# Opening of a graph-network kernel: halved first loads, the mean subtracted in the scaling, GpSimd rounding two weights

## What is computed

```
h  = relu(layernorm(x))                            # 1250 x 1024
e  = sigmoid(h @ wenc.T + benc)                    # 1250 x 500, the "encoder"
a  = segment_sum((e @ conv)[src] * edge_weight, dst) + e @ lin.T
x1 = x + a @ wdec.T + bdec
out = x1 + normalised_adjacency(src, dst) @ (relu(layernorm(x1)) @ W.T + b)
```

## Time and profile before

| | |
|---|---|
| median of 3 runs | 472.21 us (472.15 to 472.41) |
| span of the profiled execution, first to last instruction | 470.4 us |
| PE busy | 464.4 us |
| DVE busy | 284.1 us |
| ACT busy | 198.8 us |
| POOL busy | 109.3 us |
| granted TensorE clock, mean over the span | 1.000 (2.4 GHz) |

### The profile page before, as it was taken

How to read it: one execution, slowest core, us unless ns; L and a number is a source line. 1 busy time by engine, 2 the same in 40 slices (tenths; PEclk the granted TensorE clock), 3 DMA queues, 4 the chain that set the end, 5 groups by cost and what they waited for, 6 DMA issues and landing times.

```text
span 470.4 us, 7573 instructions
## 1 busy us (share of the span) xinstructions
PE 464.4 (99%) x3326; PEld 378.2 (80%) x2826; DVE 284.1 (60%) x527; ACT 198.8 (42%) x376; POOL 109.3 (23%) x102
## 2 busy tenths in 40 slices
PE   8999999999999999999999999999999999999997
PEld 6999999988899999888877785444449887777776
DVE  7999797697539259062367885994130095344443
ACT  6899976664439210142024446024342512221210
POOL 1500000000040000000013444000003599896640
PEclk9999999999999999999999999999999999999999
DMA  8620004000000134600499600733310133613113
GB/s 321 246 91 2 1 2 176 2 1 1 2 2 0 4 123 134 239 6 0 147 341 185 96 0 1 309 152 132 131 72 0 57 131 145 227 55 87 44 44 91
DMA packets 26316, 44.70 MB, mean 95 GB/s; under 512 B 15525, under 2 KB 15836, under 8 KB 25638
## 3 DMA queue, kind: packets, MB, share of 16 engines
q1 hardware_dynamic: 26024, 43.77, 28.5%
q0 software_dynamic: 224, 0.39, 0.3%
q10 hardware_dynamic: 30, 0.02, 0.0%
HBM read 27.53 MB, written 13.41 MB: 87 GB/s over the span
## 4 chain that ended last, share of the span: by engine, by line
PE 93%; DVE 4%; DMA 1%; issue 0%; SPq 0%; DVEq 0%
PE ps L1441 89%; PE ps L1445 3%; PE ps L1459 1%; DMA xn<-in_x_dram 1%; DVE zlo L1024 1%; DVE welo L1030 1%; DVE xn L1121 0%; DVE stats L965 0%; DVE stats L966 0%; PE ps L1620 0%; DVE h_all L1035 0%; DVE x1b L1434 0%; DVE kf L1090 0%; DVE mv L968 0%; DVE kb L1084 0%
## 5 line engine op out<-in xcount | busy, mean ns | idle before, releaser
L1441 PE MATMUL ps<-CT,ghi 125*128 125x500 f16 (+1 forms) x240 | 77.0, 339 | 0.0
L1441 PE MATMUL ps<-CT,glo 125*128 125x500 f16 (+1 forms) x240 | 76.9, 339 | 0.0
L1424 DVE SCALAR_TENSOR_TENSOR x1b<-ps,dsc,x1b 125x512 f32<-125x512 f32 x49 | 35.1, 746 | 34.3 <-PE ps L1441 34.2
L646 POOL TENSOR_TENSOR glo<-t,ghi 125x512 f16<-125x512 f32 x18 | 20.6, 1166 | 137.7 <-ACT t L883 137.7
L658 POOL TENSOR_TENSOR S<-U_all 128x500 f32<-128x500 f32 x25 | 31.7, 1277 | 83.8 <-DVE Blo L1398 58.8
L1441 PE MATMUL ps<-A_lo,h2hi 125*125 125x250 f32 (+1 forms) x160 | 49.1, 307 | 0.0
L1441 PE MATMUL ps<-wdhi,h_all 125*125 125x512 f32 (+1 forms) x128 | 40.4, 395 | 0.0
L1441 PE MATMUL ps<-zhi,wehi 128*125 128x250 f32 x160 | 39.4, 289 | 0.2 <-POOL wehi L619 0.2
L1441 PE MATMUL ps<-Bhi,Shi 128*125 128x512 f32 (+1 forms) x144 | 39.3, 388 | 0.0
L1441 PE MATMUL ps<-Blo,Shi 128*125 128x512 f32 (+1 forms) x144 | 39.3, 388 | 0.0
L1441 PEld LDWEIGHTS ps<-CT,ghi 125*128 125x128 f16 x240 | 23.5, 98 | 19.0 <-issue 0.3
(11 more groups left out here) (182 smaller groups left out, 1070.2 us busy)
## 6 DMA issues: line engine op xcount, KB each, us to landing
xn<-in_x_dram SPq DMA_DIRECT2D x10, 512.0 KB, 7.1
x<-in_x_dram SPq DMA_DIRECT2D x10, 512.0 KB
x_scratch<-x SPq DMA_DIRECT2D x10, 500.0 KB
x1b<-x_scratch SPq DMA_DIRECT2D x10, 500.0 KB
out_dram<-x1b SPq DMA_DIRECT2D x19, 240.0 KB
B<-in_W_dram SPq DMA_DIRECT2D x4, 1024.0 KB, 8.0
c_scratch<-C SPq DMA_DIRECT2D x10, 305.2 KB
wd<-in_wdec_dram SPq DMA_DIRECT2D x1, 2048.0 KB, 15.4
```

The source lines that it names most:

```text
L646: p.tensor_tensor(glo[k][0:PB, cs], t32[(2 * k + c) % 4][0:PB, :], ghi[k][0:PB, cs], ALU.subtract).then_inc(*glo_p.up(k, c))
L1424: v.scalar_tensor_tensor(r, ps[bank8["w", u, m]][0:PB, 0:512], scale, r, ALU.mult, ALU.add).then_inc(*term_ok.up(u, m, n))
L1441: return t.matmul(o_ap, lhsT, rhs, start=start, stop=stop)
```

## The change

- Blocks 0 and 1 of x are loaded as four half blocks, each with a semaphore, and `bn_stats` of a half waits for that half alone. The order is (0, 0), (0, 1), (1, 0), (1, 1).
- For blocks 0 and 1, `nb` is not computed. The scaling is (x - mean) * rstd, and waits for `rstd`.
- POOL waits for `rstd` of the first norm step in place of the last scaling. It rounds weights 0 and 1, each when it has landed, and then gathers.
- ACT no longer rounds weight 1. After its counting it goes straight to the four `zhi`.
- On DVE, `wenc_lo(0)` goes ahead of the statistics of block 2.
- The second warm-up has 34 matmuls in place of 45.

```diff
-WARM = (10, 45)
+WARM = (10, 34)
...
-    d_xn = [signal(f"d_xn{i}", [(k,) for k in range(i, NB, NXN)], 16) for i in range(NXN)]
+    d_xn = [signal(f"d_xn{i}", [(k,) for k in range(i if i > 1 else i + NXN, NB, NXN)], 16) for i in range(NXN)]
+    d_half = {(k, h): signal(f"d_half{k}{h}", [()], 16) for k in range(2) for h in range(2)}
...
-    norm_ok = signal("norm_ok", one(len(NORMS)))
+    norm_ok = signal("norm_ok", [(n,) for n in range(1, len(NORMS))])
...
-    whi_p = signal("whi_p", [(0,)])
-    whi_a = signal("whi_a", [(f,) for f in range(1, FB)])
+    whi_p = signal("whi_p", one(2))
+    whi_a = signal("whi_a", [(f,) for f in range(2, FB)])
+
+    def whi_ok(f):
+        return (whi_p if f < 2 else whi_a).at(f)
...
-        load_xn(0)
-        load_xn(1)
+        for (k, h), landed in d_half.items():
+            q.dma_start(xn[k][:, 512 * h:512 * h + 512], x[k][:, 512 * h:512 * h + 512]).then_inc(*landed.up())
         load_we(0)
...
-        p.wait_ge(*relu_v.at(1, 1))
-        p.wait_ge(*d_we[0].at())
-        p.tensor_copy(wehi[0][:, :, :], we32[0][:, :, :]).then_inc(*whi_p.up(0))
+        p.wait_ge(*rstd_ok.at(0))
+        for f in range(2):
+            p.wait_ge(*d_we[f].at())
+            p.tensor_copy(wehi[f][:, :, :], we32[f][:, :, :]).then_inc(*whi_p.up(f))
         for t in range(2):
             gather(t)
...
-        a.wait_ge(*d_we[1].at())
-        a.activation(wehi[1][:, 0:4, :], we32[1][:, 0:4, :], ACT.Copy)
         for k, h in FIRST:
             z_hi(k, h)
-        wenc_hi(1, 4)
         block_mean(3)
...
-            v.wait_ge(*d_xn[k % NXN].at(k))
+            v.wait_ge(*(d_half[k, 0].at() if k < 2 else d_xn[k % NXN].at(k)))
             v.bn_stats(stats[0:PB, k, 0, :], t[0:PB, 0:512])
+            if k < 2:
+                v.wait_ge(*d_half[k, 1].at())
             v.bn_stats(stats[0:PB, k, 1, :], t[0:PB, 512:1024]).then_inc(*x_seen.up(k))
...
-            v.wait_ge(*rstd_ok.at(n))
-            v.scalar_tensor_tensor(col["nb"][0:PB, cs], mv[0:PB, cs, 0], -1.0, d, ALU.mult, ALU.mult).then_inc(*norm_ok.up(n))
+            if n:
+                v.wait_ge(*rstd_ok.at(n))
+                v.scalar_tensor_tensor(col["nb"][0:PB, cs], mv[0:PB, cs, 0], -1.0, d, ALU.mult, ALU.mult
+                                       ).then_inc(*norm_ok.up(n))
...
-        v.wait_ge(*norm_ok.at(0))
+        v.wait_ge(*rstd_ok.at(0))
         for k, h in FIRST:
             part = xn[k][0:PB, 512 * h:512 * h + 512]
-            v.tensor_scalar(part, part, col["rstd"][0:PB, k:k + 1], col["nb"][0:PB, k:k + 1], ALU.mult, ALU.add
+            v.tensor_scalar(part, part, mv[0:PB, k, 0:1], col["rstd"][0:PB, k:k + 1], ALU.subtract, ALU.mult
                             ).then_inc(*relu_v.up(k, h))
         find_windows(0)
         find_windows(1)
+        wenc_lo(0)
         norm_stats(2)
-        wenc_lo(0)
```

More of the change, by code:

```diff
@@ L715, in block_var, with wenc_hi @@
                          accum_out=mv[0:PB, k, 1:2]).then_inc(*sums_ok.up(k, "var"))
-        def wenc_hi(f, k0=0):
+        def wenc_hi(f):
             a.wait_ge(*d_we[f].at())
-            a.activation(wehi[f][:, k0:KB, :], we32[f][:, k0:KB, :], ACT.Copy).then_inc(*whi_a.up(f))
+            a.activation(wehi[f][:, :, :], we32[f][:, :, :], ACT.Copy).then_inc(*whi_a.up(f))
         def z_relu(k, h):
@@ L1028, in wenc_lo @@
         def wenc_lo(f):
-            v.wait_ge(*(whi_a if f else whi_p).at(f))
+            v.wait_ge(*whi_ok(f))
             v.tensor_tensor(welo[f][:, :, :], we32[f][:, :, :], f32(wehi[f][:, :, :]), ALU.subtract).then_inc(*wlo_ok.up(f))
@@ L1477, in enc @@
             o_ap = slot_bank(s)[0:PB, 0:GN]
-            t.wait_ge(*(whi_a if f else whi_p).at(f))
+            t.wait_ge(*whi_ok(f))
             def one_pass(k, kind, start, stop):
```

## The result

| | before | after |
|---|---|---|
| median time | 472.15 us (471.89 to 472.41, 5 runs) | 474.74 us (473.62 to 475.14, 5 runs) |
| span, median | 470.2 us (469.9 to 470.3) | 472.6 us (471.5 to 473.0) |
| time outside the span | 1.9 us | 2.1 us |
| granted TensorE clock | 0.998 to 1.000 | 0.996 to 1.000 |

One more execution of it, at 1,628 us, is left out of every comparison.

What follows compares the result with a forecast made beforehand. PE is busy nearly throughout, so when DVE reaches its last `zlo` sets the time. Halved loads -0.4, no `nb` -0.2, POOL's roundings +1.75 make +1.15; 472.21 + 1.1 = 473.3 us, range 471.3 to 473.8.

Steps and rivals of the forecast that it cites:

- What bounds the kernel: Whole kernel: PE is busy 464.4 of 470.4 us, so only how early DVE reaches its last `zlo` counts.
- no idle time in which to catch up: PE behind 28.47 us: if DVE comes later, PE is later by just that.
- The halved loads: Loads of x blocks 0 and 1: second statistics of block 1 begin earlier, gain 0.4 us, between nothing and 0.64.
- the 0.24 for the later landing of the last bytes: Half loads of x: 0.24 us set as loss for pieces of 2 KB, against 0.64 saved at the most.
- the 0.6 taken as the worst case: Half loads of x: at the stores' rate for 2 KB pieces, the two blocks take 3.27 us against 2.66.
- ahead of the weights: SP's queue: two DMAs more, 0.43 us each, hidden by the backlog unless weight 1 came after 10.
- rival 3: Half loads of x: they bring nothing, landing 0.6 us later, with POOL still excluding DVE's scalings: 473.7 us; chance 0.08.
- Without `nb`: DVE before the scalings: the scaling starts where `nb` began, 0.2 us earlier, and keeps its 0.54 us.
- Warm-up, ACT, order on DVE: PE's shorter warm-up, ACT without rounding, `wenc_lo(0)` ahead of block 2's statistics: nothing each; PE waits 0.1 us.
- POOL's roundings beside the scalings: POOL and DVE exclude each other; two roundings of 1.02 us, costing 0.85 to 0.9 each, make DVE 1.75 us later.
- The sum: Whole kernel: -0.4 - 0.2 + 1.75 = +1.15 us, span 471.5, time 473.3 us.
- Scalings end near 12.8, second statistics near 6.3, PE near 29.6: Signs in the profile: DVE's four scalings, block 1's second statistics and PE's first `zlo` matmul of slot 4, in us.

Runs made afterwards that it cites:

- b3: Kernel before with only the four half loads of blocks 0 and 1 and the waits of the statistics on them; 473.38 us, ratio 1.0025.
- a2: Changed kernel with 46 warm-up matmuls in place of 34; 474.64 us, ratio 1.0054.
- e2: Kernel before with block 0 of x in two half loads and block 1 whole; 473.77 us, ratio 1.0036.
- b1: Kernel before with POOL's one rounding released by `rstd` in place of the last scaling; 472.72 us, ratio 1.001.
- b2: Kernel before with 34 warm-up matmuls in place of 45; 472.14 us, ratio 0.9999.
- b4: Kernel before with only the scaling (x - mean) * rstd, without `nb`, for blocks 0 and 1; 471.87 us, ratio 0.9994.
- a3: Changed kernel with blocks 0 and 1 of x loaded whole again; 473.53 us, ratio 1.0028.
- a5: Changed kernel with whole loads, POOL's roundings after the last scaling, block 2's statistics ahead of `wenc_lo(0)`, warm-up of 40; 472.26 us, ratio 1.0003.
- e3: Kernel before with whole x loads and weights 0 and 1 each loaded in two transfers; 472.11 us, ratio 1.0000.
- a1: Changed kernel with POOL's roundings waiting for the last of the four scalings, as before; 474.87 us, ratio 1.0047.
- d2: Kernel before with four half loads, SP issuing weight 0 and all that follows only when the last half has landed; 474.07 us, ratio 1.0043.
- e1: Kernel before with block 0 of x whole and block 1 in two half loads; 472.16 us, ratio 1.0010.
- d1: Kernel before with blocks 0 and 1 loaded in four transfers cut by partitions, keeping 4 KB rows; 473.99 us, ratio 1.0041.

## Why the prediction was wrong

**What bounds the kernel: right.** Each delay of DVE's scalings came out in the span. 0.73 us in b3 gave 0.72 at the first `zlo` matmul of slot 4 and 0.7 of span, 2.13 in a2 gave 2.09 (30.56 against 28.47) and 2.1 of span. That matmul is not always a good mark, and "no idle time in which to catch up" is not quite right: in e2 it came 2.15 later, with scalings 1.55 later and a span 1.5 longer. Nor was the load of block 1 the usual start of the chain. The profile of before has DVE waiting 0.27 us for it; in b1, b2, b4, a3, a5 and e3, with the same whole loads, DVE waited only for block 0 (until 4.4 to 4.6) and took the statistics of block 1 without a wait. The forecast could not know this from one profile.

**The halved loads: the step that failed.** "So the part is worth between nothing and 0.64 ... I put the loss at 0.24 and the gain at 0.4." It costs 1.1 to 1.2 us of span, b3 alone and a3 inside the change. The term that failed is the 0.24 for the later landing of the last bytes: they landed at 7.34 in b3, 7.47 in a2 and 7.8 in a1, 1.3 to 1.8 us behind the 6.04 of the whole block, and even the 0.6 taken as the worst case was too little. That term priced the bytes alone. It gave no price to what is queued behind the halves, which makes 1.0 us in b3 against d2. It counted the two issues more only "ahead of the weights", though they also stand ahead of the last half, which goes out at 2.16 to 2.46 where block 1 went out at 1.20; but by d2, e1 and e2 that is the smaller part. Why block 0 must be cut for the loss to appear stays open. The sum with 1.2 for the halves in place of -0.4 is 472.21 - 0.2 + 1.75 + 1.2 = 475.0; with the exclusion as measured, 474.7. No rival had the halves as a loss; rival 3, with next to nothing for them and a chance of 0.08, came nearest, at 473.7.

**Without `nb`: right.** 0.2 was forecast; the scaling starts 0.20 behind the start of `rstd`, where `nb` stood between, and b4 shows 0.3 of span.

**Warm-up, ACT, order on DVE: nothing each, nearly right.** The warm-up is shown to be worth nothing at either length. The forecast had PE waiting 0.1 for the first piece; it waits 1.30, since the first scaling is the one held. a5 shows that the two weights rounded by POOL and ACT's free start bring no span either: its 470.1 is 0.2 above b4. The order on DVE matters where POOL's second rounding comes beside `wenc_lo(0)`, as in a1; in the changed kernel it does not.

**POOL's roundings beside the scalings: right in kind, 1.48 for 1.75.** The exclusion was inferred from instructions that read two tensors and from the rate of the scaling. It is now shown for this very instruction: 1.13, 1.24 and 1.33 us beside a rounding, 0.53 to 0.54 without, in the same program with one wait changed (a1 against the changed kernel, b1 against the kernel before). The Trainium skill, page "SBUF — State Buffer", section "Who interferes with whom", has the same rule, and the runs agree. Two details were not as forecast. The first scaling was held too, though its recorded start (9.45) is 0.03 ahead of POOL's (9.48); recorded starts do not tell who wins. And the price is not a share of the rounding: a held scaling ends 0.28 us behind the rounding, in the profiles of after, a2, a3 and b1 alike, so it costs what is left of the rounding at its start, plus 0.28, less its own 0.53.

**The sum.** Halves 1.2, `nb` -0.3, the roundings 1.5: 2.4 us of span, as measured (472.6 against 470.2). About 0.2 us more lies outside the span. It is there in after, a1, a2, a3 and a5 (2.14 to 2.2 us against 1.9), and in no kernel built on before. So it comes with both roundings on POOL, none on ACT, or the signals for them; this was not taken apart.

**The profile that seemed to confirm it.** "Scalings end near 12.8, second statistics near 6.3, PE near 29.6" was answered with 12.84, 6.55 and 29.88, and a span of 471.5. All four are near, in an execution that was 1.1 us shorter than the median. That they are so near is luck, even in this execution: the halves brought 0.12 us (statistics ended at 7.24 in place of 7.36) and not 0.4, the roundings cost 1.48 and not 1.75, and the two errors cancel. Only the runs beside it showed that the loads were misjudged.

Of all the kernels, b4 is the fastest: 471.87 us, by time not told from the kernel before.

## What to carry to other kernels

Before splitting a load to start sooner, find the last byte that the chain waits for, and measure when it lands with the load split: a piece that lands early is worth nothing if the last one lands a microsecond later. Counting the issues ahead of it is not enough; e1 and e2 have the same count and lie 1.6 us apart. Keep work of GpSimd off the stretch where VectorE runs its fast one-tensor instructions on the chain, and put it beside statistics, which it leaves alone (0.68 us each beside a rounding); moving it by one wait may only hand the price to the next such instruction. Before a profile is taken as proof, its execution's time is to be compared with the other executions of the same kernel.

## What the runs showed of the hardware

- With the same four half loads, the last half landed anywhere from 6.53 us (after) to 7.8 (a1), and the spans of after went from 471.5 to 473.0. The kernel before, with whole blocks, stayed between 469.9 and 470.3 in 92 executions. Part of the spread comes with the halves: b3, with nothing but them, has 470.7 to 471.7. a3, with whole loads, has 471.1 to 472.1, so it is not the halves alone.
- From 1 to 6 us, with block 0 cut by columns and nothing held back, the DMA engines were 0.72 to 0.83 busy and moved 219 to 249 GB/s; with both blocks whole, 0.79 to 0.85 and 271 to 294. With block 1 alone cut (e1) it was 0.81 and 257, with both cut by partitions (d1) 0.83 and 177.
- A scaling that meets a rounding ends 0.28 us behind it, in the profiles of after, a2, a3 and b1, though its recorded start was 0.03 us ahead of the rounding's in three of them.
- An idle stretch of 1.06 us of PE behind the warm-up (b2) left the granted clock at 0.999 to 1.000 and the time where it was, and one of 1.30 us (the profile of after) left it at 1.00. Behind idle stretches of 2.10 us (a1) and 1.91 us (d1), with transposes one by one behind them, the clock fell to 1.2 GHz, at 12.3 and at 14.1 us.
